# Delta attention on one core: one form of the block inverse by products, its transpose by VectorE, sign changes on ScalarE, steps in a new order

## The chip, the cores and the metric

The kernel runs on one core of a Trainium2 chip. The metric is the device time of one launch in microseconds (us). A core has five engines that run side by side: TensorE (PE in the rows), VectorE (DVE), ScalarE (ACT), GpSimd (POOL) and SyncE (SP, which here only starts DMAs). Each works through its own list of instructions in order, and they wait for one another by semaphores.

## The reference, cut to what matters

The program is a chain of four layers, each an attention and a feed-forward part, on an input of 2 x 1024 tokens of width 256. Only the first attention, the delta attention, is touched by the change. For each of 16 heads of size 128 it computes q, k, v by projection, a causal convolution over 4 tokens and SiLU, per-token statistics that give a rate beta and a decay g, and then this recurrence over the tokens:

```
def step(S, inp):
    q_t, k_t, v_t, g_t, b_t = inp
    S = S * jnp.exp(g_t)[..., None]
    kv = jnp.einsum('bhk,bhkv->bhv', k_t, S)
    delta = (v_t - kv) * b_t[..., None]
    S = S + k_t[..., None] * delta[..., None, :]
    o_t = jnp.einsum('bhk,bhkv->bhv', q_t * scale, S)
    return (S, o_t)
```

The output is normalised, gated, and projected back. All data is fp32.

## The kernel before, in words

`delta_attention` cuts the work into 64 units (`NU0`): 16 heads x 4 groups of 512 tokens (`GRP`); unit u has state `St[:, u % 2]`, and `first(u)` tells that it starts from a zero state (two units in four). A unit is four chunks of 128 tokens. The recurrence inside a chunk is turned into matrix products: it needs the inverse of a unit lower triangular 128x128 matrix per chunk, here I + A, where A holds the decayed products of k with k.

A is built in seven levels (`LV` = 7). At level lv, `products(u, lv)` multiplies `kF` with `kq` into the bank `lpd`; then GpSimd scales half of `kF` and half of `kq` by the decay totals (`scale_kF`, `scale_kq`), and VectorE copies the wanted part of `lpd` under a mask (`mask`, into `MB` for levels 0 to 4, `MA` for 5 and 6; the same instruction masks the products with q). So the levels of one unit form a ring: products on PE, scaling on POOL and masking on DVE, products of the next level.

The inverse is built beside it. For blocks of 32x32 (four along the diagonal of each of four chunks, 16 in all) the kernel keeps two forms in `TB`: slot 0 and slot 1, each 128x128, one the transpose of the other block by block. At each level 1 to 4, `in_blocks` (L327 to L333, 16 matmuls of 32x32 a call) makes X from the level's matrix and slot 1, ScalarE copies X into `Xs`, a second and a third call make the update of slot 0 (`Xb, Tb(0)`) and of slot 1 (`Tb(0), Xb`), and one VectorE subtraction of 128x256 takes both off `TB`. Slot 1 is started by a call that multiplies level 0's matrix with the constant `eye`. Levels 5 and 6 join blocks into `TT` (the form that is used later) and `Tm`: the negative of the last products is written there by VectorE (L944 twice, L953, L980).

The second half of a unit is its chain of states: for each of four chunks, w (kq x St), R on DVE, dl (TT x R), Dl on ACT, s (khat x Dl), St on DVE; the outputs collect in the bank `co`.

Nothing plans the order at run time. Each engine has a loop over turns `t` with steps `if (u := unit(t, off)) is not None`, in an order written out by hand; one turn does one unit's worth of every step, for units that lie up to six turns apart. The period of a turn times 64 is the stage. SyncE loads one head's weights each four turns.

Names used further on: P0 to P6 are the `products` of levels 0 to 6; X1 to X5 the calls into columns 0 to 127 of `xy`; Y1 to Y5 the calls that update slot 0; X6 and Y6 the four 64x64 products of level 6; K, Q, V the three projections (L307); w, dl, s with a chunk number the matmuls of the state chain; vh the product with `wsv` (L538); yo the output projection (L500).

Of the kernel before, what the change touches and what calls it, by code (L numbers as in the profile page):

```python
# [17 lines left out]
P = 128  # L18
# [171 lines left out]
def delta_attention(nc, T, ins):  # L190
    with ExitStack() as c:
# [47 lines left out]
        stat_read, sT_mm, st_sums, sums_ready, roots, norms_ready = sem("stat_read"), sem("sT_mm"), sem("st_sums"), sem("sums_ready"), sem("roots"), sem("norms_ready")  # L239
        s3_ready, wo_ready, hid_ready, hid_silu, beta_in, a1_ready = sem("s3_ready"), sem("wo_ready"), sem("hid_ready"), sem("hid_silu"), sem("beta_in"), sem("a1_ready")  # L240
        beta_exp, rb_ready, al_mm, z_ready, rb_mm, kF_ready = sem("beta_exp"), sem("rb_ready"), sem("al_mm"), sem("z_ready"), sem("rb_mm"), sem("kF_ready")
        mz_ready, ez_ready, sp_ready, w_exp, w_ready, kq0_ready = sem("mz_ready"), sem("ez_ready"), sem("sp_ready"), sem("w_exp"), sem("w_ready"), sem("kq0_ready")
        kq1_ready, dg_mm, diag_ready, low0_ready, tm0_ready, tm_spread = sem("kq1_ready"), sem("dg_mm"), sem("diag_ready"), sem("low0_ready"), sem("tm0_ready"), sem("tm_spread")
        tm5_ready, tt6_ready, kh_mm, khat_ready, s0_ready, tg_mm = sem("tm5_ready"), sem("tt6_ready"), sem("kh_mm"), sem("khat_ready"), sem("s0_ready"), sem("tg_mm")
        osq_ready, og_ready, ss_mm, ms_ready, rr_ready, yo_mm = sem("osq_ready"), sem("og_ready"), sem("ss_mm"), sem("ms_ready"), sem("rr_ready"), sem("yo_mm")
# [5 lines left out]
        scaled_kq = {i: sem(f"scaled_kq_{i}") for i in (0, 1, 2, 3, 4, 6)}  # L251
        x_mm = {i: sem(f"x_mm_{i}") for i in (1, 2, 4, 5, 6)}
        xs_ready = {i: sem(f"xs_ready_{i}") for i in (1, 2, 3, 4, 5, 6)}
        tb_ready = {i: sem(f"tb_ready_{i}") for i in (1, 2, 3, 4)}
        y_mm = {i: sem(f"y_mm_{i}") for i in (2, 4, 5)}
        yt_mm = {i: sem(f"yt_mm_{i}") for i in (3, 6)}
        masked = {i: sem(f"masked_{i}") for i in (4, 5)}
        scaled_kF = {i: sem(f"scaled_kF_{i}") for i in (5,)}
        w_mm = {i: sem(f"w_mm_{i}") for i in (0, 1, 2, 3)}
        dl_mm = {i: sem(f"dl_mm_{i}") for i in (0, 1, 2, 3)}  # L260
# [3 lines left out]
        r_ready = {i: sem(f"r_ready_{i}") for i in (1, 2, 3)}  # L264
        o_mm = {i: sem(f"o_mm_{i}") for i in (3,)}

# [17 lines left out]
        TURNS = NU0 + 30  # L284

        with nc.Block() as block:
# [17 lines left out]
            def _(pe):  # L304
# [36 lines left out]
                for t in range(TURNS):  # L341
                    if (u := unit(t, 29)) is not None:
                        nc.tensor.matmul(co[:, ch_(2)], St[:, u % 2], kq[:, u % 2, 1, ch_(2)], start=True, stop=False)
                    if (u := unit(t, 28)) is not None:
# [4 lines left out]
                    if (u := unit(t, 27)) is not None:  # L349
                        if u == 0:  # L350
# [4 lines left out]
                    if (u := unit(t, 29)) is not None:  # L355
                        pe.wait_ge(r_ready[2], u + 1)
                        nc.tensor.matmul(ca[:, 0:P], TT[:, u % 2, ch_(2)], R[:, ch_(2)], start=True, stop=True).then_inc(dl_mm[2], 1)
                    if (u := unit(t, 28)) is not None:
                        pe.wait_ge(xs_ready[2], u + 1)
                        in_blocks(2 * P, Tb(0), Xb, range(NB), 0, 0)  # L360
                    if (u := unit(t, 0)) is not None:
                        if u == 0:
                            pe.wait_ge(const_loaded, 112)
                            for i, bank in enumerate((lpd, xy, ca, co)):
                                for kd in range(KD):
                                    nc.tensor.matmul(bank[:], wg1[:, kd], T.xnT[:, kd, i * GRP:(i + 1) * GRP], start=(kd == 0), stop=(kd == KD - 1))
                    if (u := unit(t, 28)) is not None:
                        in_blocks(P, Xb, Tb(0), range(NB), 0, 0).then_inc(y_mm[2], 1)
                    if (u := unit(t, 26)) is not None:
                        if u < 2:  # L370
# [3 lines left out]
                    if (u := unit(t, 29)) is not None:  # L374
                        pe.wait_ge(dl_ready[2], u + 1)
                        nc.tensor.matmul(ca[:, 0:P], khat[:, ch_(2)], Dl[:, ch_(2)], start=True, stop=True).then_inc(s_mm[2], 1)
                    if (u := unit(t, 28)) is not None:
                        pe.wait_ge(tb_ready[2], u + 1)
                        in_blocks(0, low_b(3), Tb(1), range(NB), 0, 0)
                        pe.wait_ge(scaled_kq[3], u + 1)  # L380
                        products(u, 4).then_inc(p_mm[4], 1)
                    if (u := unit(t, 26)) is not None:
# [8 lines left out]
                    if (u := unit(t, 29)) is not None:  # L391
                        pe.wait_ge(s_ready[2], u + 1)
                        nc.tensor.matmul(ca[:, 0:P], kq[:, u % 2, 0, ch_(3)], St[:, u % 2], start=True, stop=True).then_inc(w_mm[3], 1)
                    if (u := unit(t, 28)) is not None:
# [4 lines left out]
                        pe.wait_ge(xs_ready[3], u + 1)  # L399
                        in_blocks(P, Xb, Tb(0), range(NB), 0, 0)  # L400
                        in_blocks(2 * P, Tb(0), Xb, range(NB), 0, 0).then_inc(yt_mm[3], 1)
                    if (u := unit(t, 26)) is not None:
# [4 lines left out]
                    if (u := unit(t, 29)) is not None:  # L407
                        nc.tensor.matmul(co[:, ch_(2)], Dl[:, ch_(2)], MA[:, 2 + u % 2, ch_(2)], start=False, stop=True)
                        nc.tensor.matmul(co[:, ch_(3)], St[:, u % 2], kq[:, u % 2, 1, ch_(3)], start=True, stop=False)
                    if (u := unit(t, 28)) is not None:  # L410
                        pe.wait_ge(tb_ready[3], u + 1)
                        in_blocks(0, low_b(4), Tb(1), range(NB), 0, 0).then_inc(x_mm[4], 1)
                    if (u := unit(t, 25)) is not None:
# [5 lines left out]
                    if (u := unit(t, 29)) is not None:  # L419
                        pe.wait_ge(r_ready[3], u + 1)  # L420
                        nc.tensor.matmul(ca[:, 0:P], TT[:, u % 2, ch_(3)], R[:, ch_(3)], start=True, stop=True).then_inc(dl_mm[3], 1)
                    if (u := unit(t, 28)) is not None:
                        pe.wait_ge(xs_ready[4], u + 1)
                        in_blocks(2 * P, Tb(0), Xb, range(NB), 0, 0)
                        in_blocks(P, Xb, Tb(0), range(NB), 0, 0).then_inc(y_mm[4], 1)
                    if (u := unit(t, 27)) is not None:
                        if u == 0:
                            pe.wait_ge(rb_ready, u + 1)
# [3 lines left out]
                    if (u := unit(t, 28)) is not None:  # L432
                        pe.wait_ge(masked[5], u + 1)
                        pe.wait_ge(scaled_kF[5], u + 1)
                        products(u, 6).then_inc(p_mm[6], 1)
                        pe.wait_ge(tb_ready[4], u + 1)
                        in_blocks(0, next_b, Tb(1), (0, 2), 0, 1).then_inc(x_mm[5], 1)
                    if (u := unit(t, 29)) is not None:
                        pe.wait_ge(dl_ready[3], u + 1)
                        nc.tensor.matmul(co[:, ch_(3)], Dl[:, ch_(3)], MA[:, 2 + u % 2, ch_(3)], start=False, stop=True).then_inc(o_mm[3], 1)  # L440
                        nc.tensor.matmul(ca[:, 0:P], khat[:, ch_(3)], Dl[:, ch_(3)], start=True, stop=True).then_inc(s_mm[3], 1)
                    if (u := unit(t, 25)) is not None:
                        project(u, 1, W_V).then_inc(proj_v, 1)
                    if (u := unit(t, 28)) is not None:
                        pe.wait_ge(xs_ready[5], u + 1)
                        in_blocks(2 * P, Tb(0), Xb, (0,), 1, 1)
                        in_blocks(P, Xb, Tb(0), (0, 2), 1, 0).then_inc(y_mm[5], 1)
                    if (u := unit(t, 29)) is not None:
                        pe.wait_ge(kF_ready, min(u + 3, NU0))
                        pe.wait_ge(osq_ready, u + 1)  # L450
# [3 lines left out]
                    if (u := unit(t, 25)) is not None:  # L454
                        pe.wait_ge(conv_k[2], u + 1)
                        project(u, 0, W_Q).then_inc(proj_q, 1)
                    if (u := unit(t, 28)) is not None:
# [4 lines left out]
                        pe.wait_ge(tm_spread, u + 1)  # L462
                        pe.wait_ge(tm5_ready, u + 1)
                        for j in range(NC):
                            last = nc.tensor.matmul(xy[64:, j * 64:(j + 1) * 64], MA[0:64, 1, j * P + 64:(j + 1) * P], Tm[0:64, j * 64:(j + 1) * 64],
                                                    start=True, stop=True, tile_position=(0, 64), skip_group_check=True)
                        last.then_inc(x_mm[6], 1)
# [1988 lines left out]
```

## Time and profile before

| what | value |
|---|---|
| median of three runs | 5595.47 us (5595.19 to 5602.07) |
| the profiled execution: its own time | 5594.32 us |
| its span in the trace | 5592.5 us |
| delta attention in it | about 50 us to 2130 us |
| PE / DVE / ACT / POOL busy, whole span | 96% / 59% / 48% / 34% |

A fp32 matmul call stands in the trace as two PE instructions. Where a row has two times, the first is the start from the span's beginning, the second how long the group was busy; consecutive instructions on an engine overlap by some tens of nanoseconds, so the cost of a group in its engine's time is the distance from its start to the next group's start.

### The profile page before, as it was taken

The page shows a single profiled execution, that of the slowest core. Times are in us where ns is not written, and L with a number is a line of the kernel's source. Part 1 is how long each engine was busy: PE and PEld are TensorE (multiplying, and loading weights), DVE is VectorE, ACT ScalarE, POOL GpSimd, SP SyncE. Part 2 cuts the span into 40 slices and gives each one's busy share as a digit, 9 for nine tenths or more (in the row PEclk, how much of TensorE's full clock was granted, in tenths as well). Part 3 has the DMA queues.
Part 4 walks back from the last instruction along what each step waited for, and adds up shares of the span by engine and source line. Part 5 has one row for each costly group of instructions (what it writes and reads, how often), then busy time and mean ns, then how long its engine had stood idle before and what let it go on. Part 6 is the DMA issues. An engine that isn't in the chain of part 4 may idle for free. (4 is left out here: it accounts for less than half of the span.)

```text
span 5592.5 us, 159786 instructions
## 1 busy us (share of the span) xinstructions
PE 5352.9 (96%) x69266; PEld 3621.9 (65%) x69266; DVE 3326.5 (59%) x7451; ACT 2697.5 (48%) x5744; POOL 1898.1 (34%) x2352
## 2 busy tenths in 40 slices
PE   6999999999999998999999998999898999999999
PEld 3777777777777775677777754333365777667565
DVE  5888888888888884344444425766254444444222
ACT  5777677677777761355555521466611222222211
POOL 4888888878878881000000002000000111111000
PEclk9999999999999998999999998899999999999999
DMA  0000000000000000000000000000100111112100
GB/s 31 8 8 8 8 12 8 8 8 8 8 8 8 8 4 18 13 14 12 12 12 12 7 23 8 1 1 1 61 1 20 67 67 67 66 67 68 56 5 8
DMA packets 34300, 115.97 MB, mean 21 GB/s; under 512 B 4416, under 2 KB 9792, under 8 KB 33600
## 3 DMA queue, kind: packets, MB, share of 16 engines
q1 hardware_dynamic: 33600, 105.74, 5.4%
q8 instruction: 548, 8.98, 0.6%
q14 instruction: 152, 1.25, 0.1%
HBM read 103.63 MB, written 2.10 MB: 19 GB/s over the span
## 5 line engine op out<-in xcount | busy, mean ns | idle before, releaser
L700 POOL TENSOR_TENSOR d_kq<-d_kq,d_tot 128x512 f32<-128x512 f32 x448 | 526.6, 1175 | 43.7 <-PE d_lpd L324 43.7
L795 DVE SCALAR_TENSOR_TENSOR d_qkv<-d_fr,d_wts,d_qkv 128x509 f32<-128x509 f32 (+2 forms) x576 | 421.8, 741 | 25.0 <-ACT d_tail L573 21.4
L704 POOL TENSOR_TENSOR d_kF<-d_kF,d_tot 128x256 f32<-128x256 f32 x448 | 307.4, 686 | 274.0 <-PE d_lpd L318 264.6
L1975 DVE TENSOR_REDUCE r_nm<-r_ps 128x2 f32<-128x1024 f32 x256 | 307.8, 1222 | 142.5 <-PE r_ps L1794 142.3
L307 PE MATMUL d_fr<-xnT,d_wts 128*128 128x512 f32 x768 | 374.1, 610 | 6.7 <-DVE d_qkv L795 5.6
L1189 POOL TENSOR_TENSOR f1rstd<-f1var,mhalf 128x4 f32<-128x4 f32 x4 | 4.0, 1009 | 1090.3 <-DVE f1var L1214 1090.3
L2073 PE MATMUL e_pj<-xnT,e_wts 128*128 128x512 f32 x768 | 349.2, 604 | 12.7 <-DMA e_wts<-in_w3all 11.3
L1895 ACT ACTIVATE r_pT<-r_ps 128x512 f32<-128x512 f32 x512 | 274.9, 598 | 148.7 <-PE r_ps L1802 148.1
L1426 PEld LDWEIGHTS c_po<-c_pT,c_vt 128*128 128x128 f32 x2304 | 294.7, 191 | 21.0 <-ACT c_pT L1491 9.2
L1529 DVE TENSOR_TENSOR c_sc<-c_sc,c_mask 128x128 f32<-128x128 f32 x256 | 76.7, 300 | 382.8 <-PE c_sc L1381 382.8
L1426 PE MATMUL c_po<-c_pT,c_vt 128*128 128x128 f32 x2304 | 301.9, 276 | 0.2
L1794 PE MATMUL r_ps<-r_kT,r_qT 32*128 32x512 f32 x1024 | 293.8, 697 | 2.7 <-DVE r_nm L1975 1.1
L1381 PE MATMUL c_sc<-c_kT,c_qT 128*128 128x512 f32 (+3 forms) x768 | 290.2, 487 | 0.7 <-ACT c_qT L1452 0.7
L714 POOL TENSOR_TENSOR d_pw<-d_st,d_half 128x20 f32<-128x20 f32 x64 | 262.0, 4094 | 80.6 <-DVE d_st L894 80.6
L1802 PE MATMUL r_ps<-r_qT,r_kT 32*128 32x512 f32 x1024 | 279.8, 651 | 0.8 <-ACT r_pT L1895 0.8
L2073 PEld LDWEIGHTS e_pj<-xnT,e_wts 128*128 128x128 f32 x768 | 141.7, 191 | 177.4 <-issue 154.5
L1125 PE MATMUL f3pg<-xnT,f3ws 128*128 128x512 f32 x544 | 246.4, 596 | 6.7 <-DMA f3ws<-in_f3w 6.7
L2204 POOL TENSOR_TENSOR e_acc<-e_acc,e_osq 128x512 f32<-128x512 f32 x60 | 76.0, 1267 | 433.9 <-ACT e_osq L2173 433.9
L1252 DVE TENSOR_TENSOR f3hid<-f3act,f3side 128x512 f32<-128x512 f32 x68 | 46.7, 687 | 280.6 <-ACT f3act L1173 280.6
L1468 ACT ACTIVATE c_oT<-c_po 128x128 f32<-128x128 f32 x256 | 71.0, 277 | 286.0 <-PE c_po L1426 285.9
L307 PEld LDWEIGHTS d_fr<-xnT,d_wts 128*128 128x128 f32 x768 | 131.5, 191 | 105.7 <-issue 93.5
L1533 DVE TENSOR_REDUCE c_nmax<-c_sc 128x1 f32<-128x1024 f32 (+7 forms) x256 | 194.0, 758 | 9.0
(495 smaller groups left out, 13446.8 us busy)
## 6 DMA issues: line engine op xcount, KB each, us to landing
e_wts<-in_w3all SPq DMA_DIRECT2D x64, 897.0 KB, 4.5
d_wts<-in_headw SPq DMA_DIRECT2D x16, 583.5 KB, 3.8
c_wqo<-in_wqo SPq DMA_DIRECT2D x32, 256.0 KB, 2.6
f3ws<-in_f3w SPq DMA_DIRECT2D x17, 384.0 KB, 8.6
f2ws<-in_f2s SPq DMA_DIRECT2D x16, 256.0 KB, 6.2
f2qs<-in_f2q SPq DMA_DIRECT2D x16, 256.0 KB, 6.6
f1ws<-in_f1w SPq DMA_DIRECT2D x8, 384.0 KB, 6.1
f0ws<-in_f0w SPq DMA_DIRECT2D x6, 384.0 KB, 5.4
```

What stands on the lines that cost most here:

```text
L307: last = nc.tensor.matmul(fr[:, bank, :], w_of(u)[:, w0 + kd * P:w0 + (kd + 1) * P], T.xnT[:, kd, tok(u):tok(u) + GRP], start=(kd == 0), s ...
L700: return nc.gpsimd.tensor_tensor(v, v, bc(bc(by_pair(u, lv)[:, :, 0], 2, h), 1, 2), ALU.mult)
L704: return nc.gpsimd.tensor_tensor(f, f, bc(by_pair(u, lv)[:, :, 1], 2, 1 << lv), ALU.mult)
L714: nc.gpsimd.tensor_tensor(pw[:, u % 3], st[:, u % 2], bc(half[:].to_broadcast([P, 5]), 2, NC), ALU.pow).then_inc(roots, 1)
L795: return nc.vector.scalar_tensor_tensor(into, fr[:, x // 2, 0:GRP - 3 + i], tap(u, x, i), into, ALU.mult, ALU.add)
L1381: last = nc.tensor.matmul(sc[:, n % 2, k, 0:w], qT[:, h % 2, t * P:(t + 1) * P], kT[:, h // 4 % 2, k * GRP:k * GRP + w], start=True, stop= ...
L1426: last = nc.tensor.matmul(po[:, 0:P], vt[:, n // (4 * QT) % 2, j], pT[:, n % 2, j * P:(j + 1) * P], start=(j == 0), stop=(j == t))
L1794: last = nc.tensor.matmul(ps[:, r + w, :], qT[band(i0 + w), j, tok(t)], kT[band(i0 + w), j // 2, keys], start=True, stop=True, tile_positi ...
L1802: nc.tensor.matmul(ps[:, k, :], kT[band(i), jj // 2, tok(b * QT + kt)], qT[band(i), jj, (G - 1) * GRP:G * GRP], start=True, stop=True, til ...
L1895: nc.scalar.activation(pT[:, N % 3, i, :], ps[:, k, :], ACT.Exp).then_inc(cols_read, 1)
L1975: nc.vector.tensor_reduce(nm[:, t % 2, half, 4 * j + i0:4 * j + i0 + 2], ps[:, row_pair(row - 1):row_pair(row - 1) + 2], AX, ALU.max).then ...
L2073: last = nc.tensor.matmul(pj[:, x % 2, :], w[:, w0 + kd * P:w0 + (kd + 1) * P], T.xnT[:, kd, g * GRP:(g + 1) * GRP], start=(kd == 0), stop ...
```

## The change

On PE, the call with `eye` goes, and so do the calls for slot 1 at levels 1 to 4; only level 5 keeps its one (four matmuls). On VectorE, the subtraction is 128x128, of slot 0 alone, and a `transpose` (32x32 blocks within 128x128) writes slot 1 from slot 0, five times a unit. The four sign changes of levels 5 and 6 are done by ScalarE. And the steps of all four engines stand in a new order.

```diff
 # TensorE, level 0 and levels 1 to 4 (level 2 shown)
-                        pe.wait_ge(low0_ready, u + 1)
-                        in_blocks(0, low_b(0), eye_b, range(NB), 0, 0)
-                        pe.wait_ge(scaled_kq[0], u + 1)
+                        pe.wait_ge(masked[0], u + 1)
+                        pe.wait_ge(scaled_kF[0], u + 1)
                         products(u, 1).then_inc(p_mm[1], 1)
...
-                        pe.wait_ge(tb_ready[1], u + 1)
-                        in_blocks(0, low_b(2), Tb(1), range(NB), 0, 0).then_inc(x_mm[2], 1)
+                        pe.wait_ge(masked[2], u + 1)
                         pe.wait_ge(scaled_kq[2], u + 1)
                         products(u, 3).then_inc(p_mm[3], 1)
+                        pe.wait_ge(tm_ready[1], u + 1)
+                        in_blocks(0, low_b(2), Tb(1), range(NB), 0, 0).then_inc(x_mm[2], 1)
...
-                        in_blocks(2 * P, Tb(0), Xb, range(NB), 0, 0)
                         in_blocks(P, Xb, Tb(0), range(NB), 0, 0).then_inc(y_mm[2], 1)
 # VectorE
-                        nc.vector.tensor_tensor(TB[:], TB[:], xy[:, P:3 * P].rearrange("p (x i) -> p x i", x=2), ALU.subtract).then_inc(tb_ready[4], 1)
+                        nc.vector.tensor_tensor(TB[:, 0], TB[:, 0], xy[:, P:2 * P], ALU.subtract).then_inc(tb_ready[4], 1)
+                        dve.wait_ge(tb_ready[4], u + 1)
+                        nc.vector.transpose(TB[:, 1], TB[:, 0]).then_inc(tm_ready[4], 1)
...
-                        nc.vector.tensor_tensor(c3(TB[:, 1]), bc(eye[:], 1, NC), c3(xy[:, 0:P]), ALU.subtract).then_inc(tm0_ready, 1)
+                        nc.vector.transpose(TB[:, 1], TB[:, 0])
...
-                        for r in (0, 2):
-                            nc.vector.tensor_scalar(TT[band(r), u % 2]..., c3(xy[band(r), P:2 * P]), -1.0, None, ALU.mult)
-                        nc.vector.tensor_scalar(Tm[band(1)]..., c3(xy[band(1), 2 * P:3 * P]), -1.0, None, ALU.mult)
-                        nc.vector.tensor_scalar(odd(TT[0:64, u % 2], 64), mh(xy[0:64, 256:512], 64), -1.0, None, ALU.mult)
 # ScalarE, behind the copy of the Q projection
+                        act.wait_ge(yt_mm[5], u + 1)
+                        nc.scalar.activation(Tm[band(1)]..., c3(xy[band(1), 2 * P:3 * P]), ACT.Copy, scale=-1.0)
+                        act.wait_ge(y_mm[5], u + 1)
+                        for r in (0, 2):
+                            last = nc.scalar.activation(TT[band(r), u % 2]..., c3(xy[band(r), P:2 * P]), ACT.Copy, scale=-1.0)
+                        last.then_inc(tt5_ready, 1)
...
+                        act.wait_ge(yt_mm[6], u + 1)
+                        nc.scalar.activation(odd(TT[0:64, u % 2], 64), mh(xy[0:64, 256:512], 64), ACT.Copy, scale=-1.0).then_inc(tt6_ready, 1)
 # the stage's turns, and TensorE before vh
-        TURNS = NU0 + 30
+        TURNS = NU0 + 7
+                        if u >= 4:
+                            pe.wait_ge(y_read[3], u - 3)
                         nc.tensor.matmul(fr[:, 3, :], wsv[:], qkv[:, u % 3, 1], ...).then_inc(vh_mm, 1)
```

The order of one turn after the change, as far as the prediction speaks of it:

- TensorE: co 2, P3, X2, dl2, two groups of transposes, s2, Y2, P4, the statistics (7 matmuls, L388), w3, P5, X3, transposes, Y3, co 2 and co 3, K, X4, dl3, V, Y4, transposes, co 3, P6, X5, s3, Q, the two calls of Y5, sums of squares (L452), X6, transposes of `kF`, w0, P0, Y6, the diagonal products (L481), co 0, dl0, yo, co 0, P1, s0, the gate (L504), w1, X1, dl1, Y1, P2, co 1, s1, co 1, vh, w2. Before, X1 was followed by dl1 too, but w1 and X1 had a `co` matmul between them; X2 stood before P3, and P0 behind Y6.
- VectorE: behind Y1's subtraction come St, mask 2 and the first transpose; the transposes of levels 2, 3 and 4 stand behind their subtractions (level 2 with mask 4 and two others between), and level 0's stands right ahead of St0, for which w1 waits.
- GpSimd: the same instructions; the power (L714) and the first work on the next unit's statistics move from the head of the turn to its tail. Behind the scalings of levels 1, 2, 3 and 5 it waits for the next products.
- ScalarE: one SiLU and one Exp table load a unit, as before; the SiLU of `hid` stands ahead of Dl0.

## Rows read from the trace of the kernel before

**Rows 1.** The page, parts 1 and 2: engines, granted TensorE clock in 40 slices.

```profile
PE 5352.9 (96%) x69266; PEld 3621.9 (65%) x69266; DVE 3326.5 (59%) x7451; ACT 2697.5 (48%) x5744; POOL 1898.1 (34%) x2352
...
PEclk9999999999999998999999998899999999999999
```

**Rows 2.** One stretch: length, busy PE PEld DVE ACT POOL, granted clock, DMA share, GB/s.

```profile
500.00:1500.00 1000.00, 974.90 (x24428) 714.22 (x24414) 876.27 (x2273) 708.43 (x1522) 810.87 (x1038) 1.00 0.03 8
```

**Rows 3.** A group of PE in the same stretch: count, busy, mean ns, idle before.

```profile
L331 PE MATMUL d_xy<-d_eye,d_MB 32*32 32x32 f32 x992 | 14.1, 194 | 0.0
```

**Rows 4.** Timeline of PE over one turn: start, us, what, idle before.

```profile
1001.64 0.45 PE L331 MATMUL d_xy<-d_TB,d_MB 32*32 32x32 f32 x32
...
1003.70 0.45 PE L331 MATMUL d_xy<-d_Xs,d_TB 32*32 32x32 f32 x32 [0.41 <-ACT d_Xs L646]
1003.97 0.48 PE L331 MATMUL d_xy<-d_TB,d_Xs 32*32 32x32 f32 x32
...
1017.58 1.88 PE L307 MATMUL d_fr<-xnT,d_wts 128*128 128x512 f32 x4
...
1020.83 1.96 PE L307 MATMUL d_fr<-xnT,d_wts 128*128 128x512 f32 x4
1022.72 0.68 PE L465 MATMUL d_xy<-d_Tm,d_MA 64*64 64x64 f32 x8
...
1028.47 0.45 PE L331 MATMUL d_xy<-d_eye,d_MB 32*32 32x32 f32 x32
1028.85 0.46 PE L318 MATMUL d_lpd<-d_kq,d_kF 128*32 128x32 f32 x32
...
1029.57 0.39 PE L518 MATMUL d_ca<-d_St,d_kq 128*128 128x128 f32 x2
...
1030.49 0.49 PE L525 MATMUL d_ca<-d_R,d_TT 128*128 128x128 f32 x2
...
1033.98 0.45 PE L331 MATMUL d_xy<-d_TB,d_MB 32*32 32x32 f32 x32
```

**Rows 5.** Groups of DVE by shape, same stretch.

```profile
L848 DVE TENSOR_TENSOR d_TB<-d_TB,d_xy 128x256 f32<-128x256 f32 x31 | 13.1, 421 | 23.9 <-PE d_xy L331 23.9
...
L1021 DVE TENSOR_TENSOR d_TB<-d_eye,d_MB 128x128 f32<-128x128 f32 x31 | 8.8, 285 | 0.0
...
L944 DVE TENSOR_SCALAR d_TT<-d_xy 32x128 f32<-32x128 f32 x63 | 17.9, 284 | 3.2
...
L980 DVE TENSOR_SCALAR d_TT<-d_xy 64x256 f32<-64x256 f32 x31 | 12.9, 416 | 8.1 <-PE d_xy L473 8.1
...
L1029 DVE TENSOR_TENSOR d_TB<-d_eye,d_xy 128x128 f32<-128x128 f32 x31 | 10.1, 325 | 0.0
```

**Rows 6.** ACT: the block copies as a group, and the V copy's timeline row.

```profile
L594 ACT ACTIVATE d_TT<-d_TB 32x128 f32<-32x128 f32 x125 | 37.9, 303 | 1.1
...
1019.50 0.69 ACT L591 ACTIVATE d_qkv<-d_fr,d_wts 128x512 f32<-128x512 f32 x1 [0.84 <-PE d_fr L307]
```

**Rows 7.** Timeline of POOL over the same turn, and its wait in the stretch.

```profile
1006.74 1.07 POOL L700 TENSOR_TENSOR d_kq<-d_kq,d_tot 128x512 f32<-128x512 f32 x1
...
1010.42 1.06 POOL L700 TENSOR_TENSOR d_kq<-d_kq,d_tot 128x512 f32<-128x512 f32 x1 [2.00 <-PE d_lpd L324]
...
1012.59 4.11 POOL L714 TENSOR_TENSOR d_pw<-d_st,d_half 128x20 f32<-128x20 f32 x1 [0.53 <-DVE d_st L894]
...
1029.43 0.74 POOL L704 TENSOR_TENSOR d_kF<-d_kF,d_tot 128x256 f32<-128x256 f32 x1 [1.04 <-PE d_lpd L318]
...
1032.23 0.67 POOL L704 TENSOR_TENSOR d_kF<-d_kF,d_tot 128x256 f32<-128x256 f32 x1 [0.80 <-PE d_lpd L318]
...
POOL d_kF L704 <- PE d_lpd L318: 131.5, 139, 3.4
```

**Rows 8.** Timeline of DVE: two instructions of the turn.

```profile
1006.97 1.40 DVE L869 SCALAR_TENSOR_TENSOR d_lp<-d_ez 128x512 f32<-128x512 f32 x1
...
1013.22 1.42 DVE L805 SCALAR_TENSOR_TENSOR d_lp<-d_ezs,d_lp 128x512 f32<-128x512 f32 x2
```

More of the change, by code:

```diff
@@ L354, in _ @@
                         last.then_inc(al_mm, 1)
[L355 to L359, printed above, removed]
-                        in_blocks(2 * P, Tb(0), Xb, range(NB), 0, 0)
-                    if (u := unit(t, 0)) is not None:
-                        if u == 0:
[L363 to L370, printed above, removed]
+                    if (u := unit(t, 3)) is not None:
+                        if u == 0:
                             pe.wait_ge(round_v, u + 1)
@@ L453, in _ @@
                         last.then_inc(ss_mm, 1)
[L454 to L457, printed above, removed]
+                    if (u := unit(t, 5)) is not None:
+                        pe.wait_ge(masked[6], u + 1)
+                        pe.wait_ge(tt5_ready, u + 1)
+                        for j in range(NC):
+                            last = nc.tensor.matmul(xy[64:, j * 64:(j + 1) * 64], MA[0:64, 1, j * P + 64:(j + 1) * P], Tm[0:64, j * 64:(j + 1) * 64],
+                                                    start=True, stop=True, tile_position=(0, 64), skip_group_check=True)
+                        last.then_inc(x_mm[6], 1)
+                        pe.wait_ge(scaled_kF[6], u + 1)
+                        for j in range(NC):
+                            last = nc.tensor.transpose(fr[:, 3, ch_(j)], kF[:, u % 2, ch_(j)], T.ident[:])
+                        last.then_inc(kh_mm, 1)
                         if not first(u):
@@ L461, in _ @@
                             nc.tensor.matmul(ca[:, 0:P], kq[:, u % 2, 0, ch_(0)], St[:, u % 2], start=True, stop=True).then_inc(w_mm[0], 1)
[L462 to L467, printed above, removed]
-                        for j in range(NC):
-                            last = nc.tensor.transpose(fr[:, 3, ch_(j)], kF[:, u % 2, ch_(j)], T.ident[:])
-                        last.then_inc(kh_mm, 1)
+                    if (u := unit(t, 4)) is not None:
+                        pe.wait_ge(kq1_ready, u + 1)
+                        products(u, 0).then_inc(p_mm[0], 1)
+                    if (u := unit(t, 5)) is not None:
                         pe.wait_ge(xs_ready[6], u + 1)
@@ L584, in _ @@
-                    if (u := unit(t, 27)) is not None:
-                        for r in range(2):
-                            last = nc.scalar.activation(Tm[band(r)].rearrange("p (c r i) -> p c r i", c=NC, r=2)[:, :, r], c3(TB[band(r), 1]), ACT.Copy)
-                        last.then_inc(tm_spread, 1)
-                    if (u := unit(t, 24)) is not None:
-                        if not first(u):
-                            act.wait_ge(proj_v, u + 1)
-                        nc.scalar.activation(qkv[:, u % 3, 2], fr[:, 1, :], ACT.Copy, scale=tap(u, 2, 3)).then_inc(evac_v, 1)
@@ L619, in _ @@
[L619 to L622 removed]
+                    if (u := unit(t, 3)) is not None:
                         if u >= 2:
@@ L670, in _ @@
+                    if (u := unit(t, 1)) is not None:
                         if u % 4 == 0:
@@ L876, in _ @@
[L876 to L879 removed]
+                        ch.did(nc.vector.tensor_scalar(be[:], be[:], 1.0, None, ALU.add), "be_1", u)
+                        dve.wait_ge(ezs_ready[0], u + 1)
+                        ch.after("poly", u)
@@ new lines, in _ @@
+                        ch.did(factor(0), "factor[0]", u)
+                    if (u := unit(t, 4)) is not None:
+                        dve.wait_ge(y_mm[3], u + 1)
+                        ch.did(nc.vector.tensor_tensor(TB[:, 0], TB[:, 0], xy[:, P:2 * P], ALU.subtract), "tb_ready[3]", u)
+                        ch.after("tb_ready[3]", u)
+                        nc.vector.transpose(TB[:, 1], TB[:, 0]).then_inc(tm_ready[3], 1)
+                    if (u := unit(t, 2)) is not None:
+                        if u < 2:
+                            dve.wait_ge(sT_mm, u + 1)
+                        sv = fr[:, 3, :].rearrange("p (c r x) -> p r c x", c=NC, r=4)
+                        nc.vector.tensor_copy(sums[:, u % 3], sv[:, 0:3, :, 1]).then_inc(sums_ready, 1)
@@ L880, in _ @@
+                    if (u := unit(t, 5)) is not None:
                         if u >= NU0 - 1:
@@ L984, in _ @@
[L984 to L986 removed]
+                    if (u := unit(t, 1)) is not None:
                         if not first(u):
@@ new lines, in _ @@
+                    if (u := unit(t, 3)) is not None:
+                        ch.after("tt0_ready", u)
+                        nc.vector.transpose(TB[:, 1], TB[:, 0])
+                    if (u := unit(t, 4)) is not None:
+                        if not first(u):
+                            dve.wait_ge(s_mm[0], u + 1)
+                            nc.vector.scalar_tensor_tensor(St[:, u % 2], St[:, u % 2], tot[:, u % 2, tot_at[LV]:tot_at[LV] + 1], ca[:, 0:P], ALU.mult, ALU.add).then_inc(s_ready[0], 1)
```

778 lines of the change are left out of this document (389 added, 389 removed).

## The prediction

> **What bounds the kernel now.** I read the page first, then the busy time by stretch, the groups of each engine, and last the timelines of one turn. TensorE is busy 96% of the span at a granted clock of nine tenths or more of full speed almost throughout [rows 1]. Inside the stage that changes, a stretch of 1000 us has it busy 974.9 us at a granted clock of 1.00, the 2.4 GHz level, with DVE at 876, POOL at 811 and ACT at 708 [rows 2]. The subtraction of L848 is done once a unit and stands there 31 times [rows 5]: the period is 1000 / 31 = 32.26 us, and the turn from one X2 to the next took 1033.98 - 1001.64 = 32.34 us [rows 4]. In it PE is idle 25.1 / 31 = 0.81 us. The reader is to see that TensorE is the bound, that it waits little, and that VectorE follows at 28.3 us a unit, GpSimd at 26.2 and ScalarE at 22.9. The state chain is no bound, as its four rounds lie spread over the turn between other matmuls.
>
> **The change part by part, per unit.**
>
> *PE, removed.* Five calls of 16 matmuls: the one with `eye` and slot 1's at levels 1 to 4. What one costs is the distance to the next start. Within a pair of calls of the same shape it is 1003.97 - 1003.70 = 0.27 us; from the `eye` call to P1, another shape, 1028.85 - 1028.47 = 0.38 [rows 4]. The 0.11 between them belongs to the change of shape and goes only if a change of shape goes. I counted in both orders how often PE passes from one tile shape (128x128, 128x32, 32x32, 64x64) to another in a turn: 31 times before, 31 after (one saved at P1, one added where Y6 now stands between P0 and the diagonal products). So I take 5 x 0.27 = 1.35 us. The upper end is 5 x 0.38 = 1.9, if every call took a change of shape with it. The lower end is 1.35 itself: the group of the `eye` call has 14.1 / 31 = 0.45 us of busy time a unit [rows 3], overlap included, so no call is cheaper than 0.27, and only waits can eat the saving. The Trainium skill (TensorEngine Tiling (Array Packing), Key Properties) says that changing the tiling mode drains the array; the rows' 0.27 against 0.38 agree. By it, too, the saving is per matmul and not per switch, 1.35 and not 1.9.
>
> *DVE.* Out go L944 twice, L980, L953 (its shape is L944's) and L1029: 2 x 0.28 + 0.42 + 0.28 + 0.33 = 1.59 us; four subtractions go from 128x256 (0.42) to 128x128 (0.29, the like of L1021 and L1029 at 0.285 and 0.325, taken between), -0.5 [rows 5]. In come five transposes of 128x128 fp32, which no row shows. Nearest are the other 128x128 instructions, 0.285 to 0.325. Lower end 0.2 (a start-to-start distance), upper end 1.0 (below, the fourth rival). I take 0.3, so +1.5, since one 128-column pass is what the nearest rows pay. Sum -0.6: DVE stays near 27.7 us. It is not the bound, so this moves nothing by itself; but each transpose lies in a path that PE waits for (subtract, wait for its own write, transpose, next X). I laid the new order out from the durations of the turn. Slack that I find: X2 about 0.6 us, X3 over 2, X4 1.7, X5 1.0, and St0, which stands right behind level 0's transpose, 0.3 before w1. At 0.3 us each nothing is late; at 0.6 w1 is late by about 0.1.
>
> *ACT.* Gains L944's pair, L953 and L980 at its own price for such blocks, 3 x 0.30 + about 0.4 [rows 6]: 22.9 + 1.3 = 24.2 us, far below the period. What counts is where they stand: behind the copy of the Q projection. V's last matmul ended at 1017.58 + 1.88 = 1019.46 [rows 4], and its copy started at 1019.50 [rows 6], 0.04 us later. So after Q: 0.04 + 0.62 (copy, start to start) + 3 x 0.31 + 0.05 = 1.65 us until `tt5_ready`. PE has in that time only Y5 (0.52) and the sums of squares (0.92), and Q's last matmul ends 0.07 after the next group's start (1020.83 + 1.96 against 1022.72 [rows 4]): X6 comes 0.25 us late. A new wait of 0.25 (ends 0 and 0.6).
>
> *Order, other waits.* w1 to dl1 took 1030.49 - 1029.57 = 0.92 us before [rows 4], which is the path w1, R on DVE, dl1. Now one `co` matmul less lies between, some 0.70 us of PE work: +0.2. Gone is the wait of the slot pair for `Xs` (0.41 in this turn [rows 4]), as Y2 stands behind two groups of transposes and s2: -0.3 as a mean. The new wait of vh for `y_read[3]` is met some 0.2 us before PE arrives by my layout; queued behind vh are only w2 and then the next turn, and DVE's two subtractions wait for vh. I set it to 0 (end +0.4). SiLU ahead of Dl0 puts a table load and 0.42 in front of it; yo's 1.76 us on PE hide it. P3 ahead of X2 asks for `scaled_kq[2]` 0.38 us earlier: met by 0.3 us.
>
> *GpSimd.* Same instructions, 26.2 us. Its exposed waits behind levels 1, 2, 3 and 5 cost at least what they do now where PE answers at once, 0.80, about the same, 0.5 and 1.1; rows show 1.04, 0.80 and 2.00 [rows 7], and the level waits are 131.5 / 31 = 4.2 us a unit now. 26.2 + 3.2 = 29.4: below the period, yet 1.5 us below only. The long stretch from P5's end to P1, with the power of 4.11 us in it, holds 16.9 us of GpSimd work against 17.6 of PE.
>
> *Edits at nothing:* fewer turns (empty ones issue nothing), table loads (two a unit in both), SyncE's loads (same waits by meaning, 3% DMA share [rows 2]), the level 0 waits of P1, met by DVE 1.5 us ahead.
>
> *Sum.* 32.26 - 1.35 + 0.25 + 0.2 - 0.3 = 31.06; my layout, with PE's start-to-start distances of the turn added up in the new order, gives 30.6 without any wait. I take 30.95, in between and nearer to the sum. Times 64 units: 64 x (32.26 - 30.95) = 84 us. The rest of the program is the same code. Against the profiled execution: 5594.3 - 84 = 5510; the runs' median is 1 us above that execution, which I neglect.
>
> **The rivals.**
>
> 1. *Forecast:* PE stays the bound and passes on nearly all of what is removed, 5510 (5475 to 5545). For: 97.5% busy now.
> 2. *The new order also removes PE's idle time:* 30.3 us a turn, from 0.81 to near 0.2 idle: 5594 - 64 x 1.96 = 5469. Against: two new narrow places above.
> 3. *Latency takes half:* transposes at 0.6 rather than 0.3, the self-waits, and the narrow places (X6, dl1, vh) add 0.6 to 0.9 a turn: 31.7, so 5594 - 36 = 5558. For: DVE has 3 us of room in a turn of 31, of which 1.9 is one wait (before Y3's subtraction) that I can't see filled.
> 4. *Slower: transposes held up by GpSimd.* L869 reads and writes SBUF alone and took 1.40 us while a scaling ran on POOL from 1006.74, where the two of the same shape at 1013.22 took 1.42 together, under the power [rows 7, 8]. So some DVE instructions wait for GpSimd to let go. If a transpose is such a one, level 0's falls into the scaling of level 1 (up to 1.1 us), level 4's into the 1.27 us product for `kq`, level 1's into that of level 2. Then w1 is late by about 0.8 (its slack of 0.3 off 1.1), Q by 0.6 (its wait for the k convolution has 0.4 of slack), the power by 0.5: 1.9 us a turn. 32.26 - 1.35 + 1.9 + 0.15 = 32.96, so 5594 + 45 = 5639. It decides from 1.2 us of such waits a turn on, where the 1.35 less the net 0.15 are used up. Against: the many DVE instructions with a PSUM operand show no such delay. The Trainium skill (GPSIMD Engine Reference, Specifications) has GpSimd contend with DVE instructions in a two-port mode or with two SBUF inputs. L869's row agrees. A transpose has one input and by VectorE: DVE Perf Modes (The three transpose paths) takes 311 ns for 128x128 in bf16; by that rule the rival falls away, and no row here shows a transpose.
>
> **How the numbers follow.** Chances: forecast 0.56, rival 2 0.14, rival 3 0.18, rival 4 0.12. The range: 5462 (rival 2 with one PE switch cost more) to 5572 (rival 3 and a little beyond); outside lie rival 4 and the rim of the others. Within 0.2%, 11 us, which is about what a measurement of this kernel tells from no change, means 5584 to 5606: the place between rivals 3 and 4, 0.04. Slower takes most of rival 4, 0.10. Faster 0.86.
>
> **What would show it.** The period of a turn in the middle of the stage: 30.9 right; 30.3 rival 2; 31.7 rival 3; over 32.3 rival 4. PE instructions a unit fall by 160. The transposes' row: mean near 300 ns and little spread refutes rival 4; a spread up to 1 us, with `PE d_ca` waiting for DVE at w1, makes it. The wait of X6 for ACT near 0.25 us a turn and that of dl1 near 0.2 check the two new waits. GpSimd's mean wait for products should shrink from 4.2 to about 3. The forecast is wrong if PE's idle time in the stretch is over 4%, whatever the cause, or if the distance from a Y call to its next group stays at 0.6 us and more.

## The result, and the profile after

The changed kernel took 5566.20 us (median of five runs, 5555.54 to 5577.52) against 5597.16 us for the kernel before: ratio 0.994, interval 0.9928 to 0.9951. The forecast was 84 us faster; it became 31 us. The profiled execution took 5559.11 us, with a span of 5557.3 us.

The page of the changed kernel, parts 1 and 2 (compare [rows 1]):

```profile
PE 5320.7 (96%) x59026; PEld 3568.2 (64%) x59026; DVE 3251.8 (59%) x7451; ACT 2767.0 (50%) x6000; POOL 1876.5 (34%) x2352
...
PEclk8999999999999988999999998999999999999999
```

PE has 69266 - 59026 = 10240 instructions less, 160 a unit, as the change says, but its busy time fell by 32 us only. The granted clock shows why. Its mean over the whole run is 0.966, before it was 0.980. A stretch of the stage, changed kernel, in the columns of [rows 2]:

```profile
500.00:1500.00 1000.00, 972.05 (x20054) 696.52 (x20055) 863.81 (x2346) 763.82 (x1692) 824.99 (x1070) 0.98 0.03 8
```

Before, this clock was 1.00. TensorE is as busy as ever, but part of its time runs at 1.2 instead of 2.4 GHz. I summed the trace's record of the granted clock over the stage, its filling and draining included: 40 us at the half clock before, 171 us after. From the first vh matmul to the last the sums are 20 and 136 us, and in turns 3 to 59 alone, the middle of the stage, 7 and 102 us. I then took the distance from one vh to the next as the turn, and set apart those turns in which the record shows no half clock (turns 3 to 59):

| | mean turn, all 63 | undisturbed turns | their mean | half clock in the stage |
|---|---|---|---|---|
| before | 31.72 us | 54 | 31.92 us | 40 us |
| changed | 31.13 us | 38 | 30.65 us | 171 us |

(The mean of all turns lies below that of the undisturbed ones in the kernel before because the first two, in the filling of the pipeline, take 21 and 27 us.) At full clock a turn became 1.27 us shorter; the forecast said 1.31. Over the 63 turns that would be 80 us, and 36.6 came. A fit over the turns gives 0.36 us for each microsecond at half clock, and the 116 us more of it between the first vh and the last (136 against 20) make 42 of the 43 that are missing. From the profile's start to the first vh the changed kernel gains 9.1 us, from the last vh to the end it loses 10.5: -36.6 - 9.1 + 10.5 = -35.2, the difference of the spans.

What a fall does is seen in PE's timeline of two turns. First an undisturbed one of the changed kernel, from the Q projection (L309, first row) to behind the output projection yo (L503):

```profile
650.81 1.88 PE L309 MATMUL d_fr<-xnT,d_wts 128*128 128x512 f32 x4
...
653.14 1.05 PE L451 MATMUL d_fr<-ones,d_osq 128*128 128x1 f32 x8
654.47 0.65 PE L457 MATMUL d_xy<-d_Tm,d_MA 64*64 64x64 f32 x8 [0.28 <-ACT d_TT L672]
655.05 0.66 PE L462 MATMUL d_fr<-ident,d_kF 128*128 128x128 f32 x4
655.63 0.46 PE L320 MATMUL d_lpd<-d_kq,d_kF 128*32 128x32 f32 x32
656.03 0.67 PE L474 MATMUL d_xy<-d_TT,d_Xs 64*64 64x64 f32 x8
656.63 0.46 PE L480 MATMUL d_fr<-d_qkv,d_kF 128*32 128x32 f32 x32
657.26 0.46 PE L491 MATMUL d_ca<-d_R,d_TT 128*128 128x128 f32 x2 [0.17 <-ACT d_TT L679]
657.56 1.95 PE L503 MATMUL d_fr<-d_wo,d_og 128*128 128x256 f32 x8
659.35 0.38 PE L507 MATMUL d_co<-d_MA,d_Dl 128*128 128x128 f32 x2
```

Then a turn in which the record has the half clock from 869.2 to 876.0:

```profile
868.14 0.65 PE L457 MATMUL d_xy<-d_Tm,d_MA 64*64 64x64 f32 x8 [0.21 <-ACT d_TT L672]
...
872.18 3.66 PE L503 MATMUL d_fr<-d_wo,d_og 128*128 128x256 f32 x8
875.64 0.56 PE L507 MATMUL d_co<-d_MA,d_Dl 128*128 128x128 f32 x2
```

yo takes 875.64 - 872.18 = 3.46 us from start to the next start, and 659.35 - 657.56 = 1.79 otherwise: twice the time. Between Q's end (652.7) and yo's start lie 4.9 us in which no matmul has more than 128 columns: the 32x32 blocks of Y5, one-column products (the sums of squares, L451), 64x64 blocks, four transposes of `kF` (L462), products with 32 columns, dl0 (L491), in other turns also w0, and two waits. I call this small work; a projection's matmul has 512 columns, one of yo 256. In the kernel before Y5 and the sums stood ahead of Q, whose end is X6's start, 1022.72 [rows 4], and yo came here:

```profile
1025.54 1.92 PE L500 MATMUL d_fr<-d_wo,d_og 128*128 128x256 f32 x8
```

That is 2.8 us. All 19 falls in turns 3 to 59 of the changed kernel begin between 1.0 and 3.6 us before yo starts: inside this stretch. Of the two in those turns of the kernel before, neither lies there. So two theories went into the experiments. Theory A, place: the clock falls for the long stretch of small work that the new order makes behind Q. Theory B, amount: it falls because a turn holds 80 matmul calls less. A third reading has to be kept in view too: that not the small work but TensorE's waits in the stretch, 0.28 and 0.17 us above and none in the kernel before, bring the clock down. The Trainium skill (TensorE: Matmul & The Clock Gate, Why this matters for your kernels) warns of long idle gaps between bursts of matmuls if the clock is to stay up. The longest idle time of PE in the stretch above is 0.28 us, and the clock fell in the like of it all the same; by that rule alone it would not have. Here the measurement decides.

The slowest and the fastest of the five transposes on VectorE in the changed kernel (group rows; compare [rows 5]):

```profile
L945 DVE STREAM_TRANSPOSE d_TB<-d_TB 128x128 f32<-128x128 f32 x32 | 10.0, 312 | 1.1
...
L1033 DVE STREAM_TRANSPOSE d_TB<-d_TB 128x128 f32<-128x128 f32 x32 | 9.5, 297 | 0.0
```

And who waited for whom from 500 to 1500 us (total, times, longest):

```profile
PE d_xy L457 <- ACT d_TT L672: 8.0, 33, 0.3
...
PE d_lpd L320 <- POOL d_kF L709: 7.6, 11, 0.7
...
PEld d_ca L527 <- DVE d_R L1051: 5.4, 32, 0.2
...
PE d_lpd L326 <- POOL d_kq L705: 4.5, 6, 0.8
```

### The profile page after: what moved, and what is told of

Read it like the earlier page. It is cut to its first block and busy times, and to the rows that moved or that the text cites. A ratio compares the mean times of both kernels' runs of the same rounds, so it can differ in the third digit from the quotient of the medians.

```text
span 5557.3 us, 139424 instructions
## 1 busy us (share of the span) xinstructions
PE 5320.7 (96%) x59026; PEld 3568.2 (64%) x59026; DVE 3251.8 (59%) x7451; ACT 2767.0 (50%) x6000; POOL 1876.5 (34%) x2352
## 5 line engine op out<-in xcount | busy, mean ns | idle before, releaser
L309 PE MATMUL d_fr<-xnT,d_wts 128*128 128x512 f32 x768 | 366.4, 601 | 11.6 <-DVE d_qkv L802 6.3
L309 PEld LDWEIGHTS d_fr<-xnT,d_wts 128*128 128x128 f32 x768 | 133.2, 193 | 109.8 <-issue 95.5
```

The lines of the kernel that those rows point to most:

```text
L309: last = nc.tensor.matmul(fr[:, bank, :], w_of(u)[:, w0 + kd * P:w0 + (kd + 1) * P], T.xnT[:, kd, tok(u):tok(u) + GRP], start=(kd == 0), s ...
```

## The experiments

Twelve runs. The kernel before ran beside e1 to e4 at 5609.6 us, beside e5 to e8 at 5605.2 and beside e9 to e12 at 5603.2; each kernel is judged by its ratio to it. "Undisturbed" and "half clock" are taken as above, "of it, turns 3 to 59" leaves filling and draining out. "Stretch" is the median distance, over turns 3 to 59, from the end of the last projection matmul to yo's start, "idle" TensorE's mean idle time in it. Before the change these were 2.75 and 0.00 us, in the changed kernel 5.04 and 0.30. The expectations of e1 to e4 were written with other sums of the half clock, 179 us for the changed kernel and 34 for the one before, where the table above has 171 and 40.

| kernel | us | ratio (interval) | undisturbed turn | stretch | idle | half clock | of it, turns 3 to 59 |
|---|---|---|---|---|---|---|---|
| e1 calls back | 5647.18 | 1.0065 (1.0048 to 1.0082) | 31.77 | 5.37 | 0.28 | 249 | 191 |
| e2 split Q | 5517.47 | 0.9836 (0.9821 to 0.9850) | 30.66 | 3.28 | 0.08 | 64 | 7 |
| e3 old order, transposes | 5510.29 | 0.9821 (0.9807 to 0.9836) | 30.61 | 2.75 | 0.00 | 48 | 0 |
| e4 fill of four, ahead of X6 | 5531.26 | 0.9859 (0.9845 to 0.9874) | 31.02 | 5.55, filled | 0.09 | 34 | 0 |
| e5 fill of four, ahead of P6 | 5587.06 | 0.9968 (0.9951 to 0.9985) | 31.11 | 5.10 | 0.31 | 173 | 109 |
| e6 fill of one, ahead of X6 | 5529.79 | 0.9872 (0.9857 to 0.9887) | 30.70 | 5.11, filled in part | 0.06 | 113 | 58 |
| e7 sign changes on VectorE | 5572.68 | 0.9937 (0.9915 to 0.9959) | 30.85 | 5.68 | 0.62 | 189 | 140 |
| e8 e3 and an earlier copy of X2 | 5503.03 | 0.9819 (0.9803 to 0.9836) | 30.39 | 2.75 | 0.02 | 49 | 5 |
| e9 e8 with the sums behind Q | 5545.08 | 0.9895 (0.9880 to 0.9910) | 31.16 | 3.95 | 0.18 | 53 | 1 |
| e10 e8 with Y5 and the sums behind Q | 5720.79 | 1.0204 (1.0187 to 1.0221) | 33.06 | 6.06 | 0.75 | 284 | 212 |
| e11 the changed kernel again | 5561.70 | 0.9924 (0.9904 to 0.9944) | 30.64 | 5.04 | 0.30 | 135 | 92 |
| e12 e8 again | 5496.39 | 0.9809 (0.9794 to 0.9823) | 30.43 | 2.75 | 0.02 | 34 | 0 |

The trace and its half clock are of one execution of each kernel. The mean granted clock of every execution, over the whole program, is on record too: 0.978 to 0.982 for the kernel before (28 executions beside the experiments), 0.964 to 0.971 for the changed kernel (nine), 0.962 to 0.968 for e1, 0.965 to 0.977 for e5, 0.974 to 0.979 for e6, 0.968 to 0.975 for e7, 0.960 to 0.963 for e10, and 0.977 to 0.983 for e2, e3, e4, e8, e9 and e12.

**e1, calls back.**

```diff
+                        in_blocks(2 * P, Tb(0), Xb, range(NB), 0, 0)
                         in_blocks(P, Xb, Tb(0), range(NB), 0, 0).then_inc(y_mm[2], 1)   # and levels 1, 3, 4
```

> The changed kernel with slot 1's four calls of 16 matmuls (levels 1 to 4) put back in front of each Y call; nobody reads what they write. Theory A (place): the granted clock falls because of the stretch of TensorE work with few columns between the Q projection and the output projection, in which X6, dl0 and the sums of squares lie; the calls lie elsewhere, so the half-clock time in the stage stays near 179 us, and the undisturbed turn grows by 4 x 0.27 = 1.1 from 30.65 to 31.7 us: 5566 + 69 = 5635 us. Theory B (amount): the clock falls because a turn holds fewer matmuls; with them back it stays up as in the kernel before (34 us at half clock): 5635 - 42 = 5593 us.

Measured: the undisturbed turn grew by 1.12 us, 0.28 a call. The half-clock time did not fall. Theory B is refuted: the amount of matmuls brings nothing back when they stand elsewhere. That it stands at 249 us and not at 171 is not a safe rise: the profiled execution was the slowest of four (clock 0.962), and the other three, at 0.967 and 0.968, lie where the changed kernel lies. The stretch is no cause of it either: in undisturbed turns it is 5.04 us as in the changed kernel, and the median of 5.37 is longer because in 32 turns the half clock itself draws it out.

**e2, split Q.**

```diff
-                        project(u, 0, W_Q).then_inc(proj_q, 1)
+                        half_project(u, 0, W_Q, 0)
...   (behind the sums of squares)
+                        half_project(u, 0, W_Q, 1).then_inc(proj_q, 1)
...   (ScalarE: the sign changes of level 5 ahead of the copy of Q)
```

> The changed kernel with the Q projection's second matmul moved behind the sums of squares, and ScalarE's sign changes of level 5 ahead of its copy of Q. Theory A (place): the stretch with few columns shrinks from 4.9 to about 3.5 us and the falls of the clock go (half-clock time from 179 to under 60 us); the wait of X6 (0.28 us a turn) goes too: 5566 - 42 - 18 = 5506 us. Theory B (amount): as many matmuls as in the changed kernel, so half-clock time stays near 179 us, and only the wait goes: 5548 us.

Measured: half clock 64 us, a little over A's bound of 60, with one fall in turns 3 to 59, and 5517 us, nearer to A's 5506. The undisturbed turn stayed at 30.66: X6's wait is gone, but P1 now waits for GpSimd's `scaled_kF[0]` 12.0 us in the 1000, 0.37 a turn. The edit breaks up the small work and takes the wait out of it at once, so it does not tell the two apart.

**e3, the old order with the five transposes.** The kernel before, with the five calls gone and, at each level:

```diff
-                        nc.vector.tensor_tensor(TB[:], TB[:], xy[:, P:3 * P]..., ALU.subtract).then_inc(tb_ready[1], 1)
+                        ch.did(nc.vector.tensor_tensor(TB[:, 0], TB[:, 0], xy[:, P:2 * P], ALU.subtract), "tb1", u)
+                        ch.after("tb1", u)
+                        nc.vector.transpose(TB[:, 1], TB[:, 0]).then_inc(tb_ready[1], 1)
```

> The kernel before with its own order of steps and sign changes on VectorE, but with the five calls taken out and slot 1 written by five VectorE transposes. Theory A (place): between Q and the output projection stands what stood there before, so the clock stays up (about 34 us at half clock); the undisturbed turn is 31.92 - 1.35 plus waits for the longer path subtract, transpose of 0 to 0.5 us, 30.6 to 31.1 us: 5511 to 5545 us. Theory B (amount): the falls come as in the changed kernel, some 40 us more: 5553 to 5585 us. A third theory, that the new order is what brings the gain and the old one stalls on the transposes, expects an undisturbed turn of 31.5 us or more.

Measured: 30.61 us undisturbed, 48 us at half clock, 5510 us. The algorithm alone, in the old order and with the sign changes where they were, brings 99 us (ratio 0.9821); the changed kernel, at 0.9940 and 0.9924, keeps 31 to 42 of it. At full clock the two orders are alike, 30.61 and 30.65 us a turn. The third theory is refuted.

**e4, a fill ahead of X6.**

```diff
                         pe.wait_ge(masked[6], u + 1)
+                        for j in range(4):
+                            nc.tensor.matmul(lpd[:, ch_(j)], T.ident[:], T.ident[:], start=True, stop=True)
                         pe.wait_ge(tt5_ready, u + 1)
```

> The changed kernel with four 128x128 fp32 matmuls more a turn (0.22 us each, 0.86 us), into the idle bank lpd, in the place where TensorE waits 0.28 us ahead of X6; nobody reads them. Theory A (place): they break the stretch with few columns, the clock stays up, and the turn pays 0.86 - 0.28 = 0.6 us: 5566 - 42 + 37 = 5561 us, with half-clock time under 60 us in the stage. Theory B (amount of 32x32 work, or the length of the turn): clock as in the changed kernel, 5603 us.

Measured: 34 us at half clock, and faster than the changed kernel with four more matmuls a turn in it. No turn from 3 to 59 has a fall. The turn at full clock grew by 0.37, not 0.58, and the time is 30 us below A's 5561. Its windows row, to set beside the one of e5 below:

```profile
200.00:2000.00 1800.00, 1776.19 (x36731) 1283.88 (x36730) 1548.69 (x4236) 1382.63 (x3060) 1487.65 (x1931) 1.00 0.03 7
```

**e5, the same fill elsewhere.** The same two lines, ahead of P6.

> The changed kernel with the same four extra 128x128 matmuls a turn as in the fill ahead of X6, but ahead of P6, between the V and the Q projection. Theory A (place): the stretch behind Q stays as it is in the changed kernel, so the half-clock time stays near 170 us in the stage, and the four cost their full 0.86 us a turn: 30.65 + 0.86 = 31.5 undisturbed, 5566 + 55 = 5621 us or, on the chip of the last runs, some 10 us more. Theory C (any more full-size work in a turn keeps the clock up): under 60 us at half clock and about 5580 us.

Measured: 173 us at half clock, as in the changed kernel, and 5587 us in place of 5621. With e4 this is the cleanest pair: the same work, in one place it keeps the clock up, in the other it doesn't. Over all ten executions (5568 to 5615 us) the clock has a median of 0.9725, above the changed kernel's 0.966 and far from e4's 0.9805, so a part of the effect that theory C expects is not excluded. The turn grew by 0.46, not 0.86: in the changed kernel P1 waits for GpSimd 0.24 us a turn (7.6 / 32 above), and that wait was gone here, which covers 0.24 of the 0.40 us between them.

```profile
200.00:2000.00 1800.00, 1765.02 (x35446) 1279.81 (x35438) 1499.70 (x4103) 1341.07 (x2965) 1426.25 (x1865) 0.97 0.03 7
```

**e6, a fill of one.** As e4 with `range(1)`.

> The changed kernel with one extra 128x128 matmul (0.22 us) in the place where TensorE waits 0.28 us ahead of X6. Theory A (place): it costs nothing, the undisturbed turn stays at 30.65 us, and the half-clock time falls in part, from about 170 to somewhere between 40 and 130 us: 5520 to 5555 us. Theory B or C: one small matmul changes nothing, 5566 us.

Measured: as A expected, 113 us at half clock at a nearly unchanged turn, ratio 0.9872 against 0.9924 for the changed kernel in e11. This run also bears on the waits. X6's is gone, and what is left in the stretch is dl0's (waits of PE, 500 to 1500 us):

```profile
PE d_ca L493 <- ACT d_TT L681: 2.2, 13, 0.2
```

That is 0.06 us a stretch, and still the clock fell nine times in turns 3 to 59, eight of them in the stretch. So waits alone are not the cause.

**e7, the sign changes on VectorE.** L672 and its like on ScalarE out; behind `og` and behind `conv_q[1]` on VectorE:

```diff
+                        dve.wait_ge(y_mm[5], u + 1)
+                        for r in (0, 2):
+                            nc.vector.tensor_scalar(TT[band(r), u % 2]..., c3(xy[band(r), P:2 * P]), -1.0, None, ALU.mult)
+                        nc.vector.tensor_scalar(Tm[band(1)]..., c3(xy[band(1), 2 * P:3 * P]), -1.0, None, ALU.mult).then_inc(tt5_ready, 1)
```

> The changed kernel with the four sign changes back on VectorE (behind og, and behind the second step of q's convolution); all else as changed. By my account ScalarE's sign changes behind its copy of Q make TensorE wait 0.28 us ahead of X6: that wait goes, the undisturbed turn falls by 0.2 to 0.3 us to 30.4 if VectorE's 1.3 us more are hidden, and as the stretch behind Q gets shorter the half-clock time falls somewhat: 5525 to 5550 us. The rival, that VectorE is short of room and makes others late, expects an undisturbed turn of 30.9 us or more and 5575 us.

Measured: a miss for my expectation, and near the rival's 30.9 us and 5575 us. X6 waits no more, but P0 waits for VectorE's `kq` instead (a wait of PE, 500 to 1500 us), and dl0 another 5.1 us in all:

```profile
PE d_lpd L320 <- DVE d_kq L985: 10.6, 31, 0.4
```

The undisturbed turn is 30.85, 0.2 longer than with ScalarE: in this order the move of the signs is worth 0.2 us a turn at full clock, too little to show in the time (0.9937 against 0.9940 and 0.9924). The stretch grew to 5.68, and the half clock did not shrink.

**e8, e3 with ScalarE's copy of X2 one step earlier**, ahead of the wait for `err_ready`.

> The old order with the five transposes, and ScalarE's copy of X2 moved one step up, ahead of the square of the error, which waits for VectorE. In the old order with transposes TensorE waited 12.7 us in 31 turns, 0.41 a turn, for that copy. If the wait goes and nothing else is late, the undisturbed turn falls from 30.61 to 30.25 us and the time from 5510 to 5487 us; if the path through s2, X3 or the statistics is late instead, it stays within 10 us of 5510.

Measured: the turn fell by 0.22 of the 0.36 us expected, from 30.61 to 30.39. In time no gain is clear of the noise: 7 us of the 23, and by the ratio 0.9819 (0.9809 in e12) against 0.9821.

**e9 and e10, the stretch made long in the old order.** e9 moves the sums of squares behind Q, e10 Y5 as well; nothing else.

> The old order with transposes and the earlier copy of X2, and one thing moved: the sums of squares (eight short instructions of TensorE, 0.9 us) stand behind the Q projection and no longer ahead of it, so that the stretch between Q and the output projection grows from 2.8 to 3.7 us. Theory A (place): the half-clock time in the stage rises from 49 us, to between 60 and 170 us, and the time by half of that: 5510 to 5560 us, where VectorE's later ms may add up to 0.3 us a turn (19 us). Rival D (the clock falls for another trait of the new order, not for this stretch): half-clock time stays near 49 us and the time within 20 us of 5503.

> The same with Y5 behind Q too, as in the changed kernel: the stretch between Q and the output projection is then 4.3 us and more, and X6 waits for VectorE's sign changes (some 0.5 us a turn more). Theory A (place): half-clock time of 150 to 260 us in the stage, 5503 + 32 + about 70 = 5600 us. Rival D: near 49 us, and 5535 us.

Measured: e9 kept its clock (53 us), against A's lower bound of 60, with a stretch of 3.95. On the clock it thus came out as rival D says; in time it lies 42 us over 5503, outside D's 20. Nearly all of its 49 us over e12 is the undisturbed turn, (31.16 - 30.43) x 64 = 47, since Q waits there for VectorE's convolution and X1 for the transpose of level 0 (waits of PE, 500 to 1500 us):

```profile
PE d_fr L307 <- DVE d_qkv L791: 13.5, 32, 0.5
PE d_xy L331 <- DVE d_TB L1034: 12.3, 16, 0.8
PE d_ca L490 <- DVE d_TT L984: 5.5, 16, 0.4
```

The third row is dl0's wait in the stretch: it comes in every other turn, at 0.3 us or more as long as X6's in the changed kernel, and the clock stayed up. With e6 this parts the small work from the waits: e6 has falls with hardly a wait, e9 has waits and no fall in its stretch. e10, with 6.06, has 284 us at half clock, in the kernel that had 34 without the move: theory A in the old order. Its undisturbed turn, 33.06, is much longer than I expected, as Q waits 27.6 us in 1000 there, and the time, 5721, is 121 us over the expectation. Its stretch also has 0.75 us of waits, so e10 alone would not tell small work from waits. That the length of the stretch, and no other trait of the new order, brings the clock down rests on e10 and e4 against e5 together, and e4 against e5 is the cleaner half.

**e11 and e12, both on one chip.**

> The changed kernel once more, for a comparison on one chip with the two moved orders: half-clock time near 170 us in the stage, about 10 us above its first time if this chip is like those of the other runs (kernel before at 5605 to 5610 us): 5576 us.

> The old order with transposes and the earlier copy of X2, on the same chip as the changed kernel: 5503 us, 70 us below the changed kernel, of which (31.13 - 30.27) x 64 = 55 lie in the turns.

Measured: 5561.70 and 5496.39 us, 65 us apart, 54 in the profiled executions. Of these, 49 lie between the first vh and the last: 13 in the undisturbed turns (30.64 against 30.43), and 99 us more at half clock there, at the fit's 0.36, make the other 36. Over 200 to 2000 us the granted clock was 0.97 in e11 and 1.00 in e12.

e12 is the fastest version measured, with e3 and e8 inside its interval: the new algorithm in the old order, 1.9% faster than the kernel before.

## Why the prediction was wrong, point by point

- *PE's five calls, 1.35 us.* Right for the four that e1 puts back: 1.12 / 4 = 0.28 a call for 0.27.
- *Transposes at 0.3 us, DVE not the bound.* Right: 0.297 to 0.312. Rival 4 is refuted: of 64 transposes on each of the five lines none took over 0.314 us, whatever GpSimd did. The subtraction from `eye` (two inputs in SBUF) took up to 0.93 us against a median of 0.28, and the scalings of GpSimd are the likely reason, not a shown one. The rule of the Trainium skill that the prediction cited (GPSIMD Engine Reference, Specifications), contention with two SBUF inputs or a two-port mode, agrees with both.
- *X6's new wait of 0.25, dl1's of 0.2.* Right: 8.0 / 33 = 0.24 and, as a wait of dl1's weight load, 5.4 / 32 = 0.17.
- *GpSimd not late at P1.* Off by a little: the slack was none, and P1 waits 0.24 us a turn. GpSimd's own waits for products did not shrink as foreseen either: 131.5 + 21.1 us for 31 turns before, 63.3 + 42.3 + 40.0 for 32 after, 4.9 and 4.6 us a turn.
- *The turn.* 31.06 by the sum and 30.95 taken, from a base of 32.26; measured 30.65 from 31.92. The base came from 31 counts in 1000 us, which is too coarse by 0.3; the difference held, 1.31 and 1.27. A part of that is luck: the sum had no term for P1's 0.24 nor for 0.14 ahead of products that wait for `kq` (4.5 / 32), and none for the idle time that the profile puts down to issue ahead of the block calls and narrow products, which shrank from (7.2 + 6.9) / 31 = 0.45 to (0.2 + 3.7) / 32 = 0.12 us a turn. These nearly cancel, so that TensorE's idle time, about 0.8 us a turn, stayed what it was.
- *"PE stays the bound and passes on nearly all of what is removed".* This step failed. It took the 1.00 of [rows 2] as a constant of the stage. The new order put Y5, the sums of squares and a new wait behind Q; the small work there grew from 2.8 to 4.9 us at a stretch, and the clock began to fall in about one turn of three. 136 us at half clock in place of 20, between the first vh and the last, gave back 43 of the 80 us at full clock. e4 against e5 shows the place; e2, e3 and e10 agree; e6 and e9 show that the waits in the stretch are not enough to explain it.
- *Rival 3,* "latency takes half", came nearer in time, 5558 for 5566 measured, with the wrong reason: PE's waits did not grow. That the time came out inside the stated range is luck of the same kind: the range reached so far for rival 3, not for the clock. The test that I named, PE idle over 4%, did not trip (2.8%). The period of 31.1 to 31.3 lay between the marks for forecast and rival 3 and could not tell them apart; the clock row could, and I had not named it.

Left open: which of the small work counts (one-column products, blocks, the transposes of `kF`), as only e9 moves one kind alone, and its clock stayed up; whether the waits add to it; why the half clock varies so much between executions of one kernel; what made 22 us more of it outside the stage (203 against 181; 185 in e11); and why the fill ahead of P6 leaves P1 no wait.

## What to carry to other kernels

When a kernel is bound by TensorE, its clock can be part of the order of work: list where the wide matmuls stand, and how long the stretches of narrow ones between them get, before and after an edit. Test an algorithm in the old order first; here that was 99 us, and the new order hid more than half of it. A clock loss can be told apart from a wait by two cheap runs, the same useless matmuls once in the suspected stretch and once elsewhere. A fill that stands where TensorE waits also takes that wait away, so the rows of waits have to be read beside it.

## What the runs showed of the hardware that I had not expected

- The granted clock fell from 2.4 to 1.2 GHz while TensorE was 97% busy, in stretches of about 5 us in which it had matmuls of 1 to 128 columns and waits of 0.28 us at most. By kernel, the half clock in turns 3 to 59 was 0 to 7 us with 2.75 to 3.95 us between Q and yo, and 92 to 212 us with 5.04 to 6.06 us, where nothing was filled in.
- Four matmuls that nobody reads made the kernel faster: ratio 0.9859 against 0.9940 and 0.9924.
- On one chip the changed kernel's four runs spread over 24 us (e11: 5548 to 5572), against 5 us of e12 and 8 us of the kernel before in seven. The two that lay high had the lower clock, 0.964 and 0.965 against 0.968 and 0.971.
- A VectorE transpose of 128x128 fp32 in 32x32 blocks takes 0.30 to 0.31 us, about as much as the other 128x128 instructions there (0.28 to 0.35).
